# First attention: scores, maxima and exponentials for each head of a pair apart, with the query projection between the heads

## The chip, the cores and the metric

One core of a Trainium2 chip runs the whole program. The metric is the time of one execution on the device in microseconds; the kernel before took 1574.98 us (median of 3 runs, 1562.34 to 1577.71).

## The reference

Two transformer layers with adaptive layer norm on x of 8 x 256 x 128, all in float32. The change touches only the attention of the first layer: 16 heads of 64, in which every query sees 16 pooled keys (one for every segment of 16 tokens) and the keys of its own and the previous window of 128 tokens.

```
h = layernorm(x) * (1 + ca) + sa
q  = rotary(h @ w_q) * scale;  kv = rotary(h @ w_kv)
lkv = LN(kv windows, previous + own);  gkv = LN(softmax-pooled segments of kv)
sim = concat([mask(q @ gkv.T), mask(q @ lkv.T)], -1)
attn = softmax(sim, -1)
out = (attn @ concat([gkv, lkv])) @ w_out + b_out
x = x + ga * out
```

Behind it come a mixture of 4 experts (top 2), a second attention with relative positions, and a mixture of 16 experts (top 1).

## The kernel before, in words

The five engines have programs of their own, written out by hand, and meet by semaphores. The first attention works in slots, one for each of the 8 batches, plus two slots ahead of them. In a slot the 16 heads go in 8 pairs, `hp` 0 to 7. `n` is the number of the pair over all slots. The two heads of a pair, `e` 0 and 1, lie in partitions 0 to 63 and 64 to 127 of `qr` (rotated queries, two buffers) and `kT` (keys). Their scores go to the two banks of `S`, one bank for a head; `S` has no second buffer. For each of two query tiles `t` a row has 144 or 272 keys: 416 columns for a head.

In each engine's program the order is fixed:

- TensorE (`slot_program`, L549): `scores(n)` (L470; masks by an identity matmul in bf16, L478, then ten fp32 instructions, L483), the query projection of the next pair (`q_proj`, L460), a piece of other work that depends on `hp`, the values of pair n-2 (`av`, L502), the transposes of the probabilities of pair n-1 (`pT_tr`, L487), other work again. `hp` 2 has the output projection of the batch before, `hp` 3 the transposes of its normed rows (`h2T_mm`) and of the next batch but one (`hT_mm`), `hp` 4 and 5 the key and value projections, `hp` 6 and 7 the transposes of keys.
- VectorE (L998): the reciprocal of the sums of pair n-1 (L1010), the maxima of pair n (L1014, one instruction for both heads at each `t`), the rotation of the queries of pair n+1 (L1070, L1074), then work of other batches: statistics, norms, rotations, routing.
- ScalarE (L631): the normalisation of the probabilities of n-1 (L628), the four exponentials of n (L618), the copy of the values' result (L680), the copies of the transposed probabilities (L686, L687), other copies.
- POOL has the powers for the norms (L1127, L1181), the scaling of keys and values, and the scatter of rows.

`s_mm` counts finished scores, `s_max` finished maxima, `s_exp` finished exponentials. `scores(n)` waits for `q_sum` (the rotated queries) and for all four exponentials of pair n-1.

Of the kernel before, what the change touches and what calls it, by code (L numbers as in the profile page):

```python
# [24 lines left out]
ALU = mybir.AluOpType  # L25
ACT = mybir.ActivationFunctionType
X = mybir.AxisListType.X

P = 128
# [3 lines left out]
H0, DH0 = 16, 64  # L33
HP = H0 // 2
INNER = H0 * DH0
SEG = 16
NSEG = NT // SEG
# [10 lines left out]
KEYS = (NSEG + P, NSEG + 2 * P)  # L48
SCOLS = sum(KEYS)
S_AT = (KEYS[1], 0)  # L50
M_AT = (P, 0)
# [132 lines left out]
def layer0_attention(nc, io, keep):  # L184

    with ExitStack() as ctx:
# [13 lines left out]
        maskb = sb("maskb", [P, MCOLS], BF16)  # L200
        identb = sb("identb", [P, P], BF16)
# [48 lines left out]
        negmax = sb("negmax", [P, 2, TILES, 2])  # L250
# [28 lines left out]
        S = ctx.enter_context(nc.psum_tensor("S", [P, 2, 512], F32))  # L279
# [25 lines left out]
        s_mm = sem("s_mm"); s_max = sem("s_max"); s_exp = sem("s_exp")  # L305
# [5 lines left out]
        bank0 = Bank(sem("a0_full"), sem("a0_drained"), "lgT:E out:L h2T:L G:E kv00:N kv10:N kT1:E kT3:E pos:L")  # L311
        bank1 = Bank(sem("a1_full"), sem("a1_drained"), "pkT:E hT:N kv01:N router:L kv11:N gkT:E kT0:E kT2:E")
# [69 lines left out]
        def _(pe):  # L382
# [77 lines left out]
            def q_proj(n, b, bp, hp):  # L460
                if hp == 0:
                    pe.wait_ge(hq, b + 1)
                if not known_zero(n):
                    pe.wait_ge(q_rot, n)
                for s in range(2):
                    mm = pe.matmul(Q[:, s * NT:(s + 1) * NT], wq[:, s, hp * P:(hp + 1) * P], hT[:, bp, :],
                                   start=True, stop=True)
                mm.then_inc(q_mm, 1)

            def scores(n, b, bp, hp):  # L470
                if hp == 0:
                    bank1.wait_emptied(pe, "kT2", b - 1)
                    bank0.wait_emptied(pe, "kT3", b - 1)
                pe.wait_ge(q_sum, n + 1)
                if not known_zero(n):
                    pe.wait_ge(s_exp, 4 * n)
                for e, at in ((0, 0), (1, SCOLS - P)):
                    pe.matmul(S[:, e, M_AT[e]:SCOLS], identb[:], maskb[:, at:at + SCOLS - M_AT[e]], start=True, stop=False,  # L478
                              skip_group_check=True)
                for t, e, to, lo, w in ((1, 0, 0, NSEG, KEYS[1]), (1, 1, 0, 0, KEYS[1]), (0, 0, 0, NSEG, P), (0, 1, 0, 0, KEYS[0]),  # L480
                                        (0, 0, P, 0, NSEG)):
                    head = slice(e * DH0, (e + 1) * DH0)
                    mm = pe.matmul(S[:, e, S_AT[t] + to:S_AT[t] + to + w], qr[head, hp % 2, t * P:(t + 1) * P],  # L483
                                   kT[head, bp, hp, lo:lo + w], start=False, stop=(t == 0), skip_group_check=True)
                mm.then_inc(s_mm, 1)
# [63 lines left out]
            def slot_program(slot, bp):  # L549

                heads, early, late, norm = parts(slot)
                np_ = 1 - bp
                for hp in range(HP):
                    n = slot * HP + hp
                    last = heads if hp > 0 else late
                    if heads:
                        scores(n, slot, bp, hp)
                    if isinstance(slot, int) and slot == -1 and hp == HP - 1:
                        pe.wait_ge(wq_in, 16 * n_wq)
                        pe.wait_ge(cast, 2)  # L560
                        pe.wait_ge(set_up, PT_ZERO)
                    if hp < HP - 1 and heads:
                        q_proj(n + 1, slot, bp, hp + 1)
                    if hp == HP - 1 and early:
                        q_proj(n + 1, slot + 1, np_, 0)
                    if late and hp == 2:
                        out_mm(slot, slot - 1)
                    if early and hp == 4:
                        G_mm(slot, slot + 1)
                    if late and hp == 5:  # L570
                        router_mm(slot, slot - 1)
                    if early and hp == 6:
                        gkT_mm(slot, slot + 1)
                    if early and hp == 7:
                        for c in (2, 3):
                            kT_mm(slot, slot + 1, np_, c)
                    if (late if hp < 2 else heads):
                        av(n - 2, slot if hp > 1 else slot - 1, bp if hp > 1 else np_, (hp - 2) % HP)
                    if last:
                        pT_tr(n - 1, (hp - 1) % HP)  # L580
                    if early and hp == 0:
                        lgT_mm(slot, slot + 1)
                    if early and hp == 2:
                        pkT_mm(slot, slot + 1)
                    if late and hp == 3:
                        h2T_mm(slot, slot - 1)
                    if norm and hp == 3:
                        hT_mm(slot, slot + 2)
                    if norm and hp in (4, 5):
                        for k in range(2):  # L590
                            kv_mm(slot, hp - 4, k)
                    if early and hp == 6:
                        for c in (0, 1):
                            kT_mm(slot, slot + 1, np_, c)
                    if late and hp == 7:
                        pos_mm(slot, slot - 1)
# [9 lines left out]
        def _(act):  # L606
# [5 lines left out]
            act.copy(modT[:].rearrange("p m b -> p (m b)"), O[:, 0:2 * NB]).then_inc(modT_out, 1)  # L612

            def exponentials(n, hp):
                act.wait_ge(s_max, n + 1)
                for t in (1, 0):
                    for e in range(2):
                        act.activation(prob[:, hp % 2, prob_at(t, e):prob_at(t, e) + KEYS[t]],  # L618
                                       S[:, e, S_AT[t]:S_AT[t] + KEYS[t]], ACT.Exp,
                                       bias=negmax[:, hp % 2, t, e:e + 1],  # L620
                                       accum_out=Z[:, hp % 2, t, e:e + 1]).then_inc(s_exp, 1)
# [9 lines left out]
            def slot_program(slot, bp):  # L631
                heads, early, late, norm = parts(slot)
                np_ = 1 - bp
                b, l, r = slot + 1, slot - 1, slot + 2

                def keys_out(c):
                    bank, a = where[f"kT{c}"]
                    bank.wait_full(act, f"kT{c}", slot)
                    if c == 0 and not known_zero(b - 1):
                        act.wait_ge(s_mm, HP * (b - 1))  # L640
                    act.copy(kT[:, np_, 2 * c:2 * c + 2, NSEG:KEYS[1]],
                             a[:].rearrange("p (u k) -> p u k", u=2)).then_inc(bank.drained, 1)

                for hp in range(HP):
                    n = slot * HP + hp
# [13 lines left out]
                    if norm and hp in (5, 6):  # L659
                        t = hp - 5  # L660
# [51 lines left out]
        def _(dve):  # L712
# [30 lines left out]
            for l in range(2):  # L743
                dve.tensor_copy(modr[:, l, 0:384], (A0 if l == 0 else A1)[0:NB, 0:384])
                i = dve.tensor_copy(modr[:, l, 384:768], S[0:NB, l, 0:384])
# [136 lines left out]
            def pooled_keys(slot, b, bp):  # L882
                bank1.wait_full(dve, "gkT", slot)
                if not known_zero(b - 1):
                    dve.wait_ge(s_mm, HP * (b - 1))
                for at in (0, KEYS[1]):
                    for u in range(2):
                        i = dve.tensor_copy(kT[:, bp].rearrange("p (g u) k -> p g u k", u=2)[:, :, u, at:at + NSEG],
                                            A1[:, u * P:(u + 1) * P].rearrange("p (g s) -> p g s", g=4)[:, :, 0:NSEG])
                i.then_inc(bank1.drained, 1)  # L890
# [107 lines left out]
            def slot_program(slot, bp):  # L998
# [3 lines left out]
                for hp in range(HP):  # L1002
# [6 lines left out]
                            dve.wait_ge(p_norm, m - 1)  # L1009
                        dve.reciprocal(rZ[:, pb], Z[:, pb]).then_inc(z_recip, 1)  # L1010
                    if heads:
                        dve.wait_ge(s_mm, n + 1)
                        for t in (1, 0):
                            i = dve.tensor_reduce(negmax[:, hp % 2, t, :], S[:, :, S_AT[t]:S_AT[t] + KEYS[t]], X, ALU.max, negate=True)  # L1014
                        i.then_inc(s_max, 1)
                    if (heads if hp < HP - 1 else early):
                        rotate_queries(n + 1, (hp + 1) % 2)
                    if early and hp == 0:
# [46 lines left out]
            def rotate_queries(n, buf):  # L1065

                dve.wait_ge(q_mm, n + 1)
                if not known_zero(n):
                    dve.wait_ge(q_sum, n)
                dve.tensor_tensor(qt[:].rearrange("p s q -> p (s q)"), Q[:], cst("rotq"), ALU.mult).then_inc(q_rot, 1)  # L1070
                dve.wait_ge(q_rot, n + 1)
                if not (isinstance(n, int) and n < 2):
                    dve.wait_ge(s_mm, n - 1)
                dve.tensor_tensor(qr[:, buf, :], qt[:, 0, :], qt[:, 1, :], ALU.add).then_inc(q_sum, 1)  # L1074

            dve.wait_ge(const_in, 16)
# [1440 lines left out]
```

## Time and profile before

| | |
|---|---|
| median of 3 runs | 1574.98 us (1562.34 to 1577.71) |
| the profiled execution | 1569.16 us, span 1567.4 us |
| mean granted clock of TensorE | 0.88 |
| busy | TensorE 77%, weight loads 59%, VectorE 62%, ScalarE 52%, POOL 47% |
| VectorE waits for scores, 85 to 610 us | 82.0 us, 36 times |

Matmuls are pipelined and their ends are modelled, so that the start of the next instruction tells more than the length of one. An instruction of the language in fp32 is two of the profile's. A row merges consecutive instructions of one line; its shape is that of the first. P is the start of a pair's masks.

### The profile page before, as it was taken

The numbers are of one execution on the slowest core, as the hardware profiler recorded it, in microseconds if no ns is written. First come the engines' busy times: TensorE is split into PE (matmuls) and PEld (weight loads), VectorE is DVE, ScalarE is ACT, GpSimd is POOL, SyncE is SP. The second block draws the span as 40 slices with busy tenths as digits, with TensorE's granted clock in tenths as the row PEclk, the third lists the DMA queues.
The fourth block names the chain that finished last, engine by engine and source line by source line (L and its number), as shares of the span: only waits on it lengthen the run. The fifth ranks groups of instructions, "written<-read, shape, count | busy, mean of one in ns | idle before, by whom it ended". The sixth has DMA issues, their size and how long they took to land. (4 is left out here: it accounts for less than half of the span.)

```text
span 1567.4 us, 30063 instructions
## 1 busy us (share of the span) xinstructions
PE 1205.5 (77%) x9276; PEld 930.3 (59%) x9276; DVE 966.3 (62%) x2147; ACT 813.4 (52%) x2164; POOL 733.6 (47%) x732
## 2 busy tenths in 40 slices
PE   2268788977778897489889889889947987788436
PEld 0145555655555575389889889889933444444336
DVE  4586686877778753564754484474444577775633
ACT  1156565656657584366666666667622443333101
POOL 2646647383765611256556646556655233211223
PEclk7588898898989898699999999999977999888658
DMA  7500000000000000603000300000043365331135
GB/s 218 162 1 3 1 10 1 10 3 7 2 7 9 1 10 8 236 9 120 12 12 8 123 8 11 10 8 11 10 154 72 83 94 106 61 46 20 22 110 154
DMA packets 152775, 76.43 MB, mean 49 GB/s; under 512 B 99992, under 2 KB 143384, under 8 KB 152408
## 3 DMA queue, kind: packets, MB, share of 16 engines
q1 hardware_dynamic: 144696, 66.42, 16.3%
q0 software_dynamic: 3072, 6.31, 1.2%
q10 hardware_dynamic: 4896, 2.36, 0.5%
q8 instruction: 54, 0.88, 0.2%
q14 instruction: 57, 0.47, 0.1%
HBM read 54.77 MB, written 19.76 MB: 48 GB/s over the span
## 5 line engine op out<-in xcount | busy, mean ns | idle before, releaser
L1454 POOL TENSOR_TENSOR hl<-hid,hh 128x256 fp32r<-128x256 f32 x396 | 292.6, 741 | 224.1 <-ACT hh L1431 220.3
L1497 DVE SCALAR_TENSOR_TENSOR hid<-GU,gub,sg 128x256 f32<-128x256 f32 x396 | 190.3, 481 | 194.4 <-ACT sg L1425 114.7
L1325 PE MATMUL GU<-xh,wh 128*128 128x256 f32 x792 | 233.0, 294 | 42.6 <-DVE wl L1473 33.4
L1425 ACT ACTIVATE sg<-GU,gub 128x256 f32<-128x256 f32 x396 | 188.2, 475 | 121.9 <-PE GU L1327 120.4
L1326 PE MATMUL GU<-xl,wh 128*128 128x256 f32 x792 | 225.1, 284 | 0.0
L1327 PE MATMUL GU<-xh,wl 128*128 128x256 f32 x792 | 224.7, 284 | 0.0
L1325 PEld LDWEIGHTS GU<-xh,wh 128*128 128x128 f32 x792 | 151.6, 191 | 52.9 <-issue 27.8
L1431 ACT CAST hh<-hid 128x256 fp32r<-128x256 f32 x396 | 158.1, 399 | 29.7 <-DVE hid L1497 28.4
L1326 PEld LDWEIGHTS GU<-xl,wh 128*128 128x128 f32 x792 | 151.9, 192 | 0.0
L1327 PEld LDWEIGHTS GU<-xh,wl 128*128 128x128 f32 x792 | 151.9, 192 | 0.0
L628 ACT ACTIVATE prob<-prob,rZ 128x272 f32<-128x272 f32 (+1 forms) x256 | 98.9, 462 | 59.0 <-DVE rZ L1010 58.9
L1938 ACT ACTIVATE pT<-ST 128x1024 f32<-128x1024 f32 x64 | 65.5, 1023 | 111.5 <-PE ST L1768 111.5
L1325 PE MATMUL OUT<-hh,wh 128*128 128x256 f32 x396 | 113.6, 287 | 11.5 <-ACT yT L1397 10.5
L1014 DVE TENSOR_REDUCE negmax<-S 128x2 f32<-128x544 f32 (+1 forms) x128 | 69.0, 580 | 82.0 <-PE S L483 82.0
L618 ACT ACTIVATE prob<-S,negmax 128x272 f32<-128x272 f32 (+1 forms) x256 | 106.7, 426 | 22.0 <-DVE negmax L1014 21.9
L2061 DVE TENSOR_REDUCE top_now<-S 128x4 f32<-128x1024 f32 x64 | 78.2, 1223 | 55.4 <-PE S L1760 55.3
L1326 PE MATMUL OUT<-hl,wh 128*128 128x256 f32 x396 | 112.0, 283 | 0.0
L1327 PE MATMUL OUT<-hh,wl 128*128 128x256 f32 x396 | 111.8, 282 | 0.0
L1760 PE MATMUL S<-KA,QA 32*128 32x256 f32 x512 | 82.4, 444 | 13.6 <-DVE top_now L2061 10.5
L1325 PEld LDWEIGHTS OUT<-hh,wh 128*128 128x128 f32 x396 | 75.4, 190 | 15.1 <-POOL hl L1454 15.1
L1768 PE MATMUL ST<-QA,KA 32*128 32x256 f32 x512 | 83.0, 447 | 0.0
L1127 POOL TENSOR_TENSOR krs<-krs,half 128x32 f32<-128x32 f32 x8 | 43.7, 5458 | 81.2 <-DVE krs L815 81.2
(305 smaller groups left out, 2880.9 us busy)
## 6 DMA issues: line engine op xcount, KB each, us to landing
raw<-in_expert_w SPq DMA_DIRECT2D x4, 2688.0 KB, 12.3
late<-in_w SPq DMA_DIRECT2D x20, 256.0 KB, 6.3
raw<-in_expert_w SPq DMA_DIRECT2D x4, 1152.0 KB, 6.7
list<-zero SPq DMA_DIRECT2D x4, 1024.0 KB, 8.7
modb<-mod_d SPq DMA_DIRECT2D x9, 384.0 KB, 4.2
early<-rel_d SPq DMA_DIRECT2D x1, 3072.0 KB, 13.1
qkv_d<-qkv SPq DMA_DIRECT2D x48, 64.0 KB
early<-in_w SPq DMA_DIRECT2D x12, 256.0 KB, 4.2
```

The lines of the kernel that those rows point to most:

```text
L618: act.activation(prob[:, hp % 2, prob_at(t, e):prob_at(t, e) + KEYS[t]], S[:, e, S_AT[t]:S_AT[t] + KEYS[t]], ACT.Exp, bias=negmax[:, hp % ...
L628: i = act.activation(part, part, ACT.Copy, scale=rZ[:, pb, t, e:e + 1])
L1325: pe.matmul(out, lhs[0], rhs[0], start=start, stop=False, skip_group_check=True)
L1326: pe.matmul(out, lhs[0], rhs[1], start=False, stop=False, skip_group_check=True)
L1327: return pe.matmul(out, lhs[1], rhs[0], start=False, stop=stop, skip_group_check=True)
L1425: act.activation(sg[:, c % BUFS], GU[c % BUFS][:, 0:TT], ACT.Silu, bias=gub[:, GATE, e * CH0 + c:e * CH0 + c + 1]).then_inc(silu, 1)
L1431: act.copy(hh[:, d % BUFS], hid[:, d % BUFS]).then_inc(hid_hi, 1)
L1454: pool.tensor_tensor(hl[:, b], hid[:, b], hh[:, b].bitcast(F32), ALU.subtract).then_inc(hid_lo, 1)
L1497: dve.scalar_tensor_tensor(out=hid[:, c % BUFS], in0=GU[c % BUFS][:, TT:2 * TT], scalar=gub[:, UP, e * CH0 + c:e * CH0 + c + 1], in1=sg[:, ...
L1760: mm = pe.matmul(S[:, e, blk * NT:(blk + 1) * NT], QA[32 * j:32 * j + BLOCK, row % 2, g, blk * P:(blk + 1) * P], KA[32 * j:32 * j + BLOCK, ...
L1768: mm = pe.matmul(ST[:, e, blk * NT:(blk + 1) * NT], KA[32 * j:32 * j + BLOCK, row % 2, g, blk * P:(blk + 1) * P], QA[32 * j:32 * j + BLOCK ...
L2061: dve.tensor_reduce(to, S[:].rearrange("p e (q k) -> p e q k", q=2), X, ALU.max, negate=True).then_inc(s_max, 1)
```

## The change

The scores of a pair are computed for head 0 first (its mask, then 272, 128 and 16 columns), then the query projection of the next pair, then head 1 (mask, 272 and 144 columns). Each head waits only for the two exponentials of its own bank. VectorE takes four maxima for two, head by head, and ScalarE goes through the four exponentials head by head. `s_mm` and `s_max` rise by two for a pair.

```diff
@@ -467,19 +467,21 @@
                                    start=True, stop=True)
                 mm.then_inc(q_mm, 1)
 
-            def scores(n, b, bp, hp):
-                if hp == 0:
-                    bank1.wait_emptied(pe, "kT2", b - 1)
-                    bank0.wait_emptied(pe, "kT3", b - 1)
-                pe.wait_ge(q_sum, n + 1)
+            def scores(n, b, bp, hp, e):
+
+                if e == 0:
+                    if hp == 0:
+                        bank1.wait_emptied(pe, "kT2", b - 1)
+                        bank0.wait_emptied(pe, "kT3", b - 1)
+                    pe.wait_ge(q_sum, n + 1)
                 if not known_zero(n):
-                    pe.wait_ge(s_exp, 4 * n)
-                for e, at in ((0, 0), (1, SCOLS - P)):
-                    pe.matmul(S[:, e, M_AT[e]:SCOLS], identb[:], maskb[:, at:at + SCOLS - M_AT[e]], start=True, stop=False,
-                              skip_group_check=True)
-                for t, e, to, lo, w in ((1, 0, 0, NSEG, KEYS[1]), (1, 1, 0, 0, KEYS[1]), (0, 0, 0, NSEG, P), (0, 1, 0, 0, KEYS[0]),
-                                        (0, 0, P, 0, NSEG)):
-                    head = slice(e * DH0, (e + 1) * DH0)
+                    pe.wait_ge(s_exp, 4 * n - 2 + 2 * e)
+                at = (0, SCOLS - P)[e]
+                pe.matmul(S[:, e, M_AT[e]:SCOLS], identb[:], maskb[:, at:at + SCOLS - M_AT[e]], start=True, stop=False,
+                          skip_group_check=True)
+                head = slice(e * DH0, (e + 1) * DH0)
+                for t, to, lo, w in (((1, 0, NSEG, KEYS[1]), (0, 0, NSEG, P), (0, P, 0, NSEG)),
+                                     ((1, 0, 0, KEYS[1]), (0, 0, 0, KEYS[0])))[e]:
                     mm = pe.matmul(S[:, e, S_AT[t] + to:S_AT[t] + to + w], qr[head, hp % 2, t * P:(t + 1) * P],
                                    kT[head, bp, hp, lo:lo + w], start=False, stop=(t == 0), skip_group_check=True)
                 mm.then_inc(s_mm, 1)
@@ -554,7 +556,7 @@
                     n = slot * HP + hp
                     last = heads if hp > 0 else late
                     if heads:
-                        scores(n, slot, bp, hp)
+                        scores(n, slot, bp, hp, 0)
                     if isinstance(slot, int) and slot == -1 and hp == HP - 1:
                         pe.wait_ge(wq_in, 16 * n_wq)
                         pe.wait_ge(cast, 2)
@@ -563,6 +565,8 @@
                         q_proj(n + 1, slot, bp, hp + 1)
                     if hp == HP - 1 and early:
                         q_proj(n + 1, slot + 1, np_, 0)
+                    if heads:
+                        scores(n, slot, bp, hp, 1)
                     if late and hp == 2:
                         out_mm(slot, slot - 1)
                     if early and hp == 4:
@@ -612,9 +616,9 @@
             act.copy(modT[:].rearrange("p m b -> p (m b)"), O[:, 0:2 * NB]).then_inc(modT_out, 1)
 
             def exponentials(n, hp):
-                act.wait_ge(s_max, n + 1)
-                for t in (1, 0):
-                    for e in range(2):
+                for e in range(2):
+                    act.wait_ge(s_max, 2 * n + e + 1)
+                    for t in (1, 0):
                         act.activation(prob[:, hp % 2, prob_at(t, e):prob_at(t, e) + KEYS[t]],
                                        S[:, e, S_AT[t]:S_AT[t] + KEYS[t]], ACT.Exp,
                                        bias=negmax[:, hp % 2, t, e:e + 1],
@@ -637,7 +641,7 @@
                     bank, a = where[f"kT{c}"]
                     bank.wait_full(act, f"kT{c}", slot)
                     if c == 0 and not known_zero(b - 1):
-                        act.wait_ge(s_mm, HP * (b - 1))
+                        act.wait_ge(s_mm, 2 * HP * (b - 1))
                     act.copy(kT[:, np_, 2 * c:2 * c + 2, NSEG:KEYS[1]],
                              a[:].rearrange("p (u k) -> p u k", u=2)).then_inc(bank.drained, 1)
 
@@ -882,7 +886,7 @@
             def pooled_keys(slot, b, bp):
                 bank1.wait_full(dve, "gkT", slot)
                 if not known_zero(b - 1):
-                    dve.wait_ge(s_mm, HP * (b - 1))
+                    dve.wait_ge(s_mm, 2 * HP * (b - 1))
                 for at in (0, KEYS[1]):
                     for u in range(2):
                         i = dve.tensor_copy(kT[:, bp].rearrange("p (g u) k -> p g u k", u=2)[:, :, u, at:at + NSEG],
@@ -1009,10 +1013,11 @@
                             dve.wait_ge(p_norm, m - 1)
                         dve.reciprocal(rZ[:, pb], Z[:, pb]).then_inc(z_recip, 1)
                     if heads:
-                        dve.wait_ge(s_mm, n + 1)
-                        for t in (1, 0):
-                            i = dve.tensor_reduce(negmax[:, hp % 2, t, :], S[:, :, S_AT[t]:S_AT[t] + KEYS[t]], X, ALU.max, negate=True)
-                        i.then_inc(s_max, 1)
+                        for e in range(2):
+                            dve.wait_ge(s_mm, 2 * n + e + 1)
+                            for t in (1, 0):
+                                i = dve.tensor_reduce(negmax[:, hp % 2, t, e:e + 1], S[:, e, S_AT[t]:S_AT[t] + KEYS[t]], X, ALU.max, negate=True)
+                            i.then_inc(s_max, 1)
                     if (heads if hp < HP - 1 else early):
                         rotate_queries(n + 1, (hp + 1) % 2)
                     if early and hp == 0:
@@ -1070,7 +1075,7 @@
                 dve.tensor_tensor(qt[:].rearrange("p s q -> p (s q)"), Q[:], cst("rotq"), ALU.mult).then_inc(q_rot, 1)
                 dve.wait_ge(q_rot, n + 1)
                 if not (isinstance(n, int) and n < 2):
-                    dve.wait_ge(s_mm, n - 1)
+                    dve.wait_ge(s_mm, 2 * (n - 1))
                 dve.tensor_tensor(qr[:, buf, :], qt[:, 0, :], qt[:, 1, :], ALU.add).then_inc(q_sum, 1)
 
             dve.wait_ge(const_in, 16)
```

On TensorE, in the last slot, whose pairs have nothing else between them: the instructions from one pair's scores on. Before:

```order
L478 MATMUL S<-maskb,identb 128x288 [waits s_exp,q_sum]
L478 MATMUL S<-maskb,identb 128x416
L483 MATMUL S<-kT,qr 128x272 x2
L483 MATMUL S<-kT,qr 128x128
L483 MATMUL S<-kT,qr 128x144
L483 MATMUL S<-kT,qr 128x16
L466 MATMUL Q<-hT,wq 128x256 [waits q_rot]
L466 MATMUL Q<-hT,wq 128x256
```

And now:

```order
L480 MATMUL S<-maskb,identb 128x288 [waits s_exp,q_sum]
L485 MATMUL S<-kT,qr 128x272
L485 MATMUL S<-kT,qr 128x128
L485 MATMUL S<-kT,qr 128x16
L466 MATMUL Q<-hT,wq 128x256 [waits q_rot]
L466 MATMUL Q<-hT,wq 128x256
L480 MATMUL S<-maskb,identb 128x416 [waits s_exp]
L485 MATMUL S<-kT,qr 128x272
L485 MATMUL S<-kT,qr 128x144
```

The matmuls are the same ones. Those of the two heads alternated; now the projection stands between them, and head 1 has a wait of its own.

On VectorE, at the same place of the last slot, before:

```order
L1010 RECIPROCAL rZ<-Z 128x4 [waits p_norm,s_exp]
L1014 TENSOR_REDUCE negmax<-S 128x2 [waits s_mm]
L1014 TENSOR_REDUCE negmax<-S 128x2
L1070 TENSOR_TENSOR qt<-Q,const 128x512 [waits q_sum,q_mm]
L1074 TENSOR_TENSOR qr<-qt 128x256 [waits s_mm,q_rot]
```

And now:

```order
L1014 RECIPROCAL rZ<-Z 128x4 [waits p_norm,s_exp]
L1019 TENSOR_REDUCE negmax<-S 128x1 [waits s_mm]
L1019 TENSOR_REDUCE negmax<-S 128x1
L1019 TENSOR_REDUCE negmax<-S 128x1 [waits s_mm]
L1019 TENSOR_REDUCE negmax<-S 128x1
L1075 TENSOR_TENSOR qt<-Q,const 128x512 [waits q_sum,q_mm]
L1079 TENSOR_TENSOR qr<-qt 128x256 [waits s_mm,q_rot]
```

The rotation of the next pair's queries, and whatever VectorE has behind it, stands behind the maximum of head 1.

## Rows read from the trace of the kernel before

**Rows 1.** The page, section 1: busy time, share of the span, instructions.

```profile
PE 1205.5 (77%) x9276; PEld 930.3 (59%) x9276; DVE 966.3 (62%) x2147; ACT 813.4 (52%) x2164; POOL 733.6 (47%) x732
```

**Rows 2.** Waits, 85 to 610 us: us in total, times, longest.

```profile
DVE negmax L1014 <- PE S L483: 82.0, 36, 7.2
...
ACT prob L618 <- DVE negmax L1014: 21.9, 18, 9.8
...
PE S L478 <- ACT prob L618: 1.9, 5, 0.8
```

**Rows 3.** Timeline of TensorE, slot 7: start, us, operation [idle before].

```profile
583.31 0.46 PE L478 MATMUL S<-maskb,identb 128*128 128x288 bf16 x2
583.70 1.07 PE L483 MATMUL S<-kT,qr 64*128 64x272 f32 x10
584.70 1.13 PE L466 MATMUL Q<-hT,wq 128*128 128x256 f32 x4
585.76 0.69 PE L509 MATMUL O<-pT,gv 32*128 32x256 f32 x2
...
588.12 0.29 PE L478 MATMUL S<-maskb,identb 128*128 128x288 bf16 x1
```

**Rows 4.** The same in instants of 0.01 us, at 583.75, 584.10 and 585.30.

```profile
583.70 0.50 PE L483 MATMUL S<-kT,qr 64*128 64x272 f32 x2
...
583.70 0.73 PE L483 MATMUL S<-kT,qr 64*128 64x272 f32 x4
...
585.02 0.59 PE L466 MATMUL Q<-hT,wq 128*128 128x256 f32 x2
```

**Rows 5.** Timeline of VectorE, the same pair.

```profile
584.81 1.09 DVE L1014 TENSOR_REDUCE negmax<-S 128x2 f32<-128x544 f32 x2 [1.75 <-PE S L483]
585.87 0.69 DVE L1070 TENSOR_TENSOR qt<-Q,const 128x512 f32<-128x512 f32 x1
```

**Rows 6.** Busy time of the engines in that period, granted clock, DMA, GB/s.

```profile
583.31:588.12 4.81, 4.81 (x37) 3.35 (x35) 2.36 (x5) 4.35 (x16) 0.00 (x0) 1.00 0.00 0
```

**Rows 7.** VectorE's groups by shape, 85 to 612 us: busy us, mean ns.

```profile
L1014 DVE TENSOR_REDUCE negmax<-S 128x2 f32<-128x544 f32 x64 | 45.7, 714 | 82.0 <-PE S L483 82.0
...
L1014 DVE TENSOR_REDUCE negmax<-S 128x2 f32<-128x288 f32 x64 | 28.6, 446 | 0.0
```

**Rows 8.** Timeline of TensorE, slot 5, pairs 2 to 5.

```profile
443.71 0.47 PE L478 MATMUL S<-maskb,identb 128*128 128x288 bf16 x2 [0.28 <-ACT prob L618]
...
452.42 0.47 PE L478 MATMUL S<-maskb,identb 128*128 128x288 bf16 x2
...
465.15 0.68 PE L530 MATMUL A<-const,h 128*128 128x128 f32 x2 [7.75 <-DVE h L929]
...
466.06 0.79 PE L478 MATMUL S<-maskb,identb 128*128 128x288 bf16 x2
...
475.38 0.46 PE L478 MATMUL S<-maskb,identb 128*128 128x288 bf16 x2
```

**Rows 9.** Timeline of VectorE, slot 5, pairs 3 to 5.

```profile
457.34 3.59 DVE L923 TENSOR_SCALAR h<-x,mv,rs 128x128 f32 x2 [0.58 <-POOL rs L1181]
...
468.76 1.09 DVE L1014 TENSOR_REDUCE negmax<-S 128x2 f32<-128x544 f32 x2 [3.65 <-PE S L483]
...
476.88 1.09 DVE L1014 TENSOR_REDUCE negmax<-S 128x2 f32<-128x544 f32 x2 [3.84 <-PE S L483]
```

**Rows 10.** Timeline of POOL, slot 5, pair 2 to pair 3.

```profile
451.03 5.54 POOL L1127 TENSOR_TENSOR krs<-krs,half 128x32 f32<-128x32 f32 x1 [10.00 <-DVE krs L815]
```

**Rows 11.** Timelines of TensorE and VectorE, slot 5, pair 6.

```profile
482.25 0.46 PE L478 MATMUL S<-maskb,identb 128*128 128x288 bf16 x2
...
485.95 0.69 DVE L1014 TENSOR_REDUCE negmax<-S 128x2 f32<-128x544 f32 x1
```

**Rows 12.** Busy time in two stretches behind stalls; the clock stands before DMA.

```profile
466.00:468.80 2.80, 2.80 (x15) 1.91 (x12) 0.04 (x1) 2.26 (x6) 2.80 (x2) 0.50 0.00 0
...
292.80:297.00 4.20, 4.20 (x14) 2.23 (x14) 3.44 (x7) 3.19 (x12) 2.80 (x3) 0.50 0.08 33
```

## The prediction

> **What bounds the kernel now.** I read the page first: TensorE is the busiest engine, 77% of the 1567.4 us span [rows 1]. The change touches the first attention alone, roughly 85 to 610 us, so every other number comes from there. There the list of waits comes next: VectorE waits 82.0 us in 36 waits for the scores, ScalarE 21.9 us for the maxima, and TensorE's wait for the exponentials, the one that the ring is about, is 1.9 us in 5 waits [rows 2]. So the ring of scores, maxima and exponentials is closed by TensorE arriving late far more often than by TensorE being held.
>
> The timeline of one pair shows why. Call P the start of a pair's mask matmuls; here P is 583.31, and the next P is 588.12, so the period is 4.81 us [rows 3]. TensorE has no idle row in it: masks and scores to 584.70, query projection to 585.76, values and transposes to 588.12. It is busy for all 4.81 us at a granted clock of 1.00, which is 2.4 GHz, with ScalarE at 4.35 us [rows 6]. VectorE waited 1.75 us for these scores, its maximum starts at P+1.50, its rotation at P+2.56 [rows 5].
>
> The third thing to see is how the scores stream. The two heads lie in different halves of the partitions, and their matmuls run together: just after 583.70 two instructions are in flight and end within 0.50 us; four are through in 0.73. Two of the query projection, which uses all 128 rows, take 0.59 [rows 4]. So a step of 272 columns costs 0.73-0.50 = 0.23 us for both heads, about what 256 columns of one query projection instruction cost: 585.02+0.59 to 584.70+1.13, 0.22 us [rows 3, 4].
>
> The Trainium skill, in TensorEngine Tiling (Array Packing), Key Properties, says that different tiles of the array work in parallel; the trace agrees with those 0.23 us.
>
> **TensorE, per pair.** The change puts the query projection between the heads, so no score matmul has a partner. Now both heads together take 583.70 to 584.70, 1.00 us [rows 3]: 0.33 for the first step, 0.23 for its second half, two steps of 128 to 144 columns at about 0.12, and 0.19 for the rest and the emptying. A head alone has the same steps (272, 128 and 16 columns, or 272 and 144) and takes about 0.97. Two heads: 1.94, **+0.94**. A second passage from mask to scores (0.39 from the first mask to the scores, 0.29 of it columns at 2.4 GHz [rows 3]) adds 0.10; a mask behind the projection, of the same array shape, saves about that much. No row has 272 columns of one head alone: the bounds are half the pair's step (+0, if one head could stream twice as fast) and the projection's rate (+0.94). I take the upper, since a projection instruction is the nearest row.
>
> The same page says that changing the tiling mode drains the engine. The change has four such passages per pair in place of three; the page gives no time, and by that rule alone the sum would be +0.1 per pair.
>
> **VectorE.** Head 0's maximum can start early, at about P+1.3. Head 1's scores are ready at P+0.22 (first mask) +0.97+0.96 (projection) +0.27 (second mask) +0.97+0.11 = P+3.50 in place of P+1.50. The maxima now take 714 and 446 ns for 544 and 288 elements [rows 7], 1.05 ns per element; 272 and 144 elements are then 0.43 and 0.29, 0.62 with the overlap that the pair has now. The rotation starts at P+4.12 in place of 2.56: **+1.56** wherever VectorE waits for the scores. Everything behind it on VectorE waits as well. Where it comes late anyway, it pays two more instructions: 4 by 0.36 against 1.16, less two overlaps of 0.10, +0.1 to 0.2; I take 0.15. ScalarE's eight activations are the same; head 0's exponentials are earlier, head 1's end near P+5.0, in front of the new P+5.75. The added semaphore steps cost nothing that a row shows.
>
> **A whole slot** (eight pairs; the example is slot 5). Pairs are 0 to 7.
> - P of pair 2 was held 0.28 us by the exponentials [rows 8]. This wait goes: +0.94-0.28 = +0.66.
> - P2 to P3 (443.71 to 452.42) is the output projection and the rest on TensorE without a wait: +0.94.
> - P3 to P4: TensorE waits 7.75 us for the rows of the second norm [rows 8]. VectorE is late by 1.56, but idled 0.58 there for POOL's power [rows 9], which stands behind a power of 5.54 us [rows 10], itself late by what pair 2 is late: +0.98.
> - P4 to P5 (466.06 to 475.38): VectorE idles 3.65 and 3.84 us for the scores [rows 9], TensorE paces it: +0.94.
> - P5 to its rotation: +1.56.
> - Pairs 6, 7 and 0: pair 6's P is 482.25, VectorE comes at 485.95 [rows 11]. Head 1 would be ready at 485.75, and VectorE itself comes 1.56 later: hidden. Without that cover it would be 1.56 again. Left is 3 x 0.15 = +0.45.
>
> Sum: 0.66+0.94+0.98+0.94+1.56+0.45 = 5.53 us. Slots 1 to 6 make 33.2; slot 0, less regular, I take as another 5.5; slot 7 has no fill work, eight pairs by 0.94 = 7.5. Together **+46 us**. Against the profiled execution's own 1569.16 us that is 1615. That run lies 0.4% below the median of the runs, 1574.98; I add a little for that and say **1617**.
>
> **The rivals.**
> - *The ring pays (faster).* If the early maximum of head 0 lets ScalarE start sooner and one head streams at the pair's whole rate, the 21.9 us that ScalarE waits for maxima and the 2 to 3 us of TensorE's ring wait [rows 2] come back: 1569-24 = 1545. It decides as soon as ScalarE sets the period. For: ScalarE is at 4.35 of 4.81 us [rows 6]. Against: TensorE has none left at all, and head 1's maximum comes later than now, ring or not. Chance 0.05.
> - *No change.* A head alone streams twice as fast (the lower bound), head 0's early work repays the switches: 1560 to 1585. Chance 0.07.
> - *Most of it is absorbed.* VectorE's delay is taken up by its idle stretches of 3.65 and 3.84 us [rows 9], and only TensorE's own stretches count: P2 to P3 and P4 to P5 in seven slots, 13 us, and slot 7, 7.5: 1590. Against: those idle stretches end with the very scores that come late. Chance 0.13.
> - *The low clock doubles it.* Behind each long stall TensorE runs at 0.50, 1.2 GHz (466.0 to 468.8), and once for 4.2 us on end [rows 12]. If scores spread over more of it, pair 4 or pair 0 pays twice, +3 to 4 us in six or seven slots: 1640. Chance 0.13.
> - *As summed*: 1617, own range 1600 to 1632. Chance 0.62.
>
> The range of 8 in 10 leaves out the first two rivals and the far end of the fourth: 1588 to 1640. A measurement of this kernel tells about 1% from no change. Faster by over 1%: 0.05; within 1%: 0.07 and a tenth of the third, 0.08; slower: 0.87.
>
> **What would show it.** In the changed profile: query projection starts at about P+1.2 and the second mask at P+2.15; the values' first matmul at P+3.4 where it was at P+2.45; the period of slot 7's plain pairs near 5.75 for 4.81; two score instructions of 272 columns never in flight together. VectorE's maxima: 128 of about 0.43 and 128 of about 0.29 us, with a new wait of 1.5 us between the heads, and its waits for scores well above 82 us. P3 to P4 longer by 1, pairs 6 and 7 hardly changed. I would be wrong if a head alone streamed 272 columns in 0.12 us, if slot 7's period stayed under 5 us, or if time outside 85 to 610 us moved.

## The result, and the profile after

The changed kernel takes **1680.2 us** (median of 4 runs, 1665.3 to 1691.8) against 1573.9 us (median of 4 by now): ratio 1.0668, 95% interval 1.0614 to 1.0722. The forecast was 1617 us, with 1588 to 1640 as the range. The direction was right and the size not: +106 us where +46 had been summed. The profiled execution took 1674.99 us, its span is 1673.2 us.

The page, section 1, against [rows 1]:

```profile
PE 1321.2 (79%) x9276; PEld 1002.4 (60%) x9276; DVE 992.9 (59%) x2275; ACT 817.8 (49%) x2164; POOL 733.8 (44%) x732
```

TensorE is busy 116 us longer with the same 9276 matmuls. Next the pair by which the price was worked out, in slot 7, TensorE and then VectorE, against [rows 3] and [rows 5] (start, us, operation):

```profile
671.37 0.29 PE L480 MATMUL S<-maskb,identb 128*128 128x288 bf16 x1
671.59 1.07 PE L485 MATMUL S<-kT,qr 64*128 64x272 f32 x6
672.59 1.13 PE L466 MATMUL Q<-hT,wq 128*128 128x256 f32 x4
673.56 0.34 PE L480 MATMUL S<-maskb,identb 128*128 128x416 bf16 x1
673.83 0.97 PE L485 MATMUL S<-kT,qr 64*128 64x272 f32 x4
674.73 0.69 PE L511 MATMUL O<-pT,gv 32*128 32x256 f32 x2
...
677.08 0.29 PE L480 MATMUL S<-maskb,identb 128*128 128x288 bf16 x1
```

```profile
674.83 0.66 DVE L1019 TENSOR_REDUCE negmax<-S 128x1 f32<-128x272 f32 x2 [0.44 <-PE S L485]
675.40 0.68 DVE L1075 TENSOR_TENSOR qt<-Q,const 128x512 f32<-128x512 f32 x1
```

P is 671.37 and the period is 5.71 us; 4.81 before, 5.75 forecast. The values begin at P+3.36 (3.39 was summed), head 1's maximum at P+3.46 (3.50), the rotation at P+4.03 (4.12). Head 0's three score matmuls take 1.00 us, and head 1's two 0.90; before, both heads took 1.00 together. So at the full clock the model of one pair was right.

In this pair head 0's maximum waits until P+2.36 (673.73). That is the exception: in pairs 2 to 6 of slot 7 it comes at P+1.32 to P+1.33, with a wait of 1.48 us between the heads, where 1.3 and 1.5 were forecast. The next pair, with P at 677.08:

```profile
678.41 0.66 DVE L1019 TENSOR_REDUCE negmax<-S 128x1 f32<-128x272 f32 x2 [1.73 <-PE S L485]
680.54 0.66 DVE L1019 TENSOR_REDUCE negmax<-S 128x1 f32<-128x272 f32 x2 [1.48 <-PE S L485]
```

Now the two stretches that it missed. Slot 4, pairs 3 and 4, TensorE, against [rows 8], which are of slot 5 (slot 5 of the changed kernel has the same rows 83.25 us later, to 0.01 us, up to the end of the stall):

```profile
443.82 0.30 PE L480 MATMUL S<-maskb,identb 128*128 128x288 bf16 x1
...
461.53 0.69 PE L532 MATMUL A<-const,h 128*128 128x128 f32 x2 [11.83 <-DVE h L933]
...
462.43 0.45 PE L480 MATMUL S<-maskb,identb 128*128 128x288 bf16 x1
...
466.55 0.55 PE L480 MATMUL S<-maskb,identb 128*128 128x416 bf16 x1
...
476.60 0.29 PE L480 MATMUL S<-maskb,identb 128*128 128x288 bf16 x1
```

The stall is 11.83 us for 7.75. The second mask comes 4.12 us behind the first; in slot 7 it was 2.19. This is the low clock: over slot 5's P4 to P5 its mean is 0.53.

```profile
545.69:560.88 15.19, 15.19 (x56) 8.67 (x54) 3.27 (x9) 6.49 (x19) 3.49 (x2) 0.53 0.00 0
```

VectorE and POOL in that stall, against [rows 9] and [rows 10]:

```profile
449.02 3.68 DVE L779 TENSOR_SCALAR h<-xt,mv,rs 128x128 f32 x2
452.62 3.80 DVE L927 TENSOR_SCALAR h<-x,mv,rs 128x128 f32 x2
```

```profile
442.78 5.43 POOL L1132 TENSOR_TENSOR krs<-krs,half 128x32 f32<-128x32 f32 x1 [16.80 <-DVE krs L819]
448.18 0.69 POOL L1186 TENSOR_TENSOR rs<-rs,half 128x2 f32<-128x2 f32 x1
448.84 3.78 POOL L1141 TENSOR_TENSOR V<-kvc,krs 128x1024 f32<-128x1024 f32 x2
```

The two small norm instructions of L779 begin at 449.02, 0.18 us behind POOL's scaling of V. Before (slot 5), they stood in front of it and took 0.59 us for two:

```profile
456.17 0.59 DVE L775 TENSOR_SCALAR h<-xt,mv,rs 128x128 f32 x2
```

```profile
457.09 3.75 POOL L1136 TENSOR_TENSOR V<-kvc,krs 128x1024 f32<-128x1024 f32 x2
460.81 3.93 POOL L1154 TENSOR_TENSOR wk<-kvr,pk 128x1024 f32<-128x1024 f32 x2
```

The Trainium skill, GPSIMD Engine Reference, Specifications, says that POOL shares its SBUF interfaces with VectorE, with contention for VectorE instructions in a 2-port mode or with two inputs from SBUF. The trace agrees for the norm's two-input steps of 128x256, which took 2.34 us beside POOL's work and 0.43 away from it. The one-input steps took 3.68 us for two against 0.59; whether they ran in such a mode no run here shows. The rows show one thing more: beside POOL, a step lasts about as long as one instruction of POOL's, 1.88 us where POOL's two scalings of V take 3.78, and 2.34 where the next two take 4.82.

Last the clock, over all 64 pairs, of the kernel before and of the changed one (first to last P; the clock stands before DMA):

```profile
85.24:598.08 512.84, 419.66 (x2755) 293.01 (x2755) 383.01 (x785) 331.65 (x1040) 279.37 (x165) 0.90 0.02 5
```

```profile
84.78:711.15 626.37, 541.08 (x2754) 367.94 (x2755) 410.93 (x911) 336.75 (x1040) 278.30 (x165) 0.80 0.01 4
```

A mean of 0.80 over 626 us between two levels, 0.5 and 1, is 2 x 0.20 x 626 = 251 us at 1.2 GHz; before it was 2 x 0.10 x 513 = 103 us. The trace's clock records add up to 253 and 105, and these are used from here on. Not all of that time is a loss, since TensorE stands idle in part of it. Laid over its busy records, it worked for 202 us at 1.2 GHz, and for 70 before. Half of that is what the clock took, by estimate 101 us and 35, so 66 us more than before. Some of this hides behind waits. From first to last P the loss is 113.5 us; 7 us of it come back behind the last pair.

P to P, mean of slots 1 to 5, in us (read from the timelines of TensorE):

| | 0-1 | 1-2 | 2-3 | 3-4 | 4-5 | 5-6 | 6-7 | 7-0 | sum |
|---|---|---|---|---|---|---|---|---|---|
| before | 8.58 | 6.12 | 8.76 | 13.62 | 9.38 | 6.87 | 7.28 | 9.02 | 69.6 |
| changed | 9.79 | 6.79 | 9.80 | 18.60 | 14.65 | 8.09 | 7.57 | 8.92 | 84.2 |
| added | 1.21 | 0.67 | 1.04 | 4.98 | 5.27 | 1.22 | 0.29 | -0.10 | 14.6 |
| forecast | 0.15 | 0.66 | 0.94 | 0.98 | 0.94 | 1.56 | 0.15 | 0.15 | 5.5 |

Two of eight intervals hold 8.3 of the 9.1 us that the forecast lacks in each slot. Slots 0 and 6 look different: slot 0 grew by 14.2 us and slot 6 by 19.3, and in slot 6 pairs 1 and 2 hold 11.6 of them (P1 to P3 25.1 us for 13.5) and P3 to P4 only 0.6. Slot 7 grew by 7.15 us, where 7.5 were forecast.

### The profile page after: what moved, and what is told of

It reads as the page before. It is cut to its first block and busy times, and to the rows that moved or that the text cites. A ratio compares the mean times of both kernels' runs of the same rounds, so it can differ in the third digit from the quotient of the medians.

```text
span 1673.2 us, 30311 instructions
## 1 busy us (share of the span) xinstructions
PE 1321.2 (79%) x9276; PEld 1002.4 (60%) x9276; DVE 992.9 (59%) x2275; ACT 817.8 (49%) x2164; POOL 733.8 (44%) x732
## 3 DMA queue, kind: packets, MB, share of 16 engines
q1 hardware_dynamic: 144696, 66.42, 15.2%
q10 hardware_dynamic: 4896, 2.36, 0.5%
## 5 line engine op out<-in xcount | busy, mean ns | idle before, releaser
L1019 DVE TENSOR_REDUCE negmax<-S 128x1 f32<-128x272 f32 (+1 forms) x256 | 82.1, 366 | 189.9 <-PE S L485 189.9
L485 PEld LDWEIGHTS S<-kT,qr 64*128 64x128 f32 x640 | 119.0, 220 | 66.6 <-issue 48.8
L485 PE MATMUL S<-kT,qr 64*128 64x272 f32 (+3 forms) x640 | 157.4, 380 | 0.0
L1330 PE MATMUL OUT<-hh,wh 128*128 128x256 f32 x396 | 113.5, 287 | 10.8 <-ACT yT L1402 9.8
```

The lines of the kernel that those rows point to most:

```text
L1019: i = dve.tensor_reduce(negmax[:, hp % 2, t, e:e + 1], S[:, e, S_AT[t]:S_AT[t] + KEYS[t]], X, ALU.max, negate=True)
L1330: pe.matmul(out, lhs[0], rhs[0], start=start, stop=False, skip_group_check=True)
```

## The experiments

There are 4 to 10 runs of each. The ratio is to the kernel before, run beside it (medians of 1567.6 to 1573.9 us). "1.2 GHz" is the time at the lower level from first to last P, and "working" the part of it in which TensorE was busy, both in us and both from the one profiled execution; the last column is slot 7's plain period. In the edits `...` marks what is left out.

| kernel | us | ratio (95%) | 1.2 GHz | working | period |
|---|---|---|---|---|---|
| before | 1573.9 | 1 | 105 | 70 | 4.81 |
| changed | 1680.2 | 1.0668 (1.0614 to 1.0722) | 253 | 202 | 5.71 |
| e1_grouped | 1611.0 | 1.0252 (1.0195 to 1.0308) | 173 | 141 | 5.27 |
| e2_pe_only | 1708.1 | 1.0865 (1.0826 to 1.0905) | 290 | 230 | 6.56 |
| e3_split_vector | 1573.3 | 1.0001 (0.9966 to 1.0036) | 139 | 104 | 4.81 |
| e4_partners | 1637.5 | 1.0402 (1.0333 to 1.0470) | 126 | 73 | 5.72 |
| e5_before_warm | 1551.3 | 0.9915 (0.9876 to 0.9953) | 59 | 52 | 4.81 |
| e6_after_warm | 1662.4 | 1.0560 (1.0479 to 1.0640) | 155 | 147 | 5.71 |
| e7_after_early_norm | 1662.4 | 1.0572 (1.0487 to 1.0657) | 232 | 202 | 5.71 |
| e8_after_early_norm_warm | 1635.7 | 1.0415 (1.0336 to 1.0493) | 134 | 129 | 5.71 |
| e9_after_early_norm_warm8 | 1614.7 | 1.0266 (1.0209 to 1.0322) | 88 | 82 | 5.71 |
| e10_before_hold | 1564.5 | 0.9958 (0.9925 to 0.9991) | 117 | 97 | 4.81 |
| e11_before_hold_weigh | 1568.4 | 0.9964 (0.9927 to 1.0001) | 110 | 100 | 4.81 |
| e12_after_hold_weigh | 1619.4 | 1.0317 (1.0257 to 1.0378) | 154 | 145 | 5.71 |

### Which part of the change costs

**e1_grouped**

```diff
-for t, e, to, lo, w in ((1, 0, 0, NSEG, KEYS[1]), (1, 1, 0, 0, KEYS[1]), (0, 0, 0, NSEG, P), (0, 1, 0, 0, KEYS[0]), (0, 0, P, 0, NSEG)):
+for t, e, to, lo, w in ((1, 0, 0, NSEG, KEYS[1]), (0, 0, 0, NSEG, P), (0, 0, P, 0, NSEG), (1, 1, 0, 0, KEYS[1]), (0, 1, 0, 0, KEYS[0])):
```

> The kernel before, with one change: behind both masks, head 0's three score matmuls are issued in a row and then head 1's two, with the query projection behind them as before. Theory (the two heads stream together only while their matmuls alternate): scores take 1.7 us in place of 1.0, slot 7's plain period goes from 4.81 to about 5.5 us, the whole is slower by 4 to 6%. Rival (the place of the query projection is what costs): period 4.8, no change. Rival (a head alone streams at the pair's rate): no change.

The same matmuls in another order cost 2.5%. In slot 7 the scores take from 634.36 to 635.82:

```profile
634.36 1.54 PE L483 MATMUL S<-kT,qr 64*128 64x272 f32 x10
635.82 1.13 PE L466 MATMUL Q<-hT,wq 128*128 128x256 f32 x4
```

That is 1.46 us for 1.00. I had expected 1.7: I had counted nothing of head 1 that can run beside head 0's last matmuls, and its first, of 272 columns, starts 0.01 us behind head 0's of 128, at 634.93. The ratio fell short of the 4 to 6% as well. The alternation is worth 0.46 us per pair without the query projection, and both rivals fall. The changed kernel's period is 0.44 us longer still: with the projection between the heads nothing of head 1 runs beside head 0 at all.

**e2_pe_only**

```diff
-pe.wait_ge(s_exp, 4 * n - 2 + 2 * e)
+pe.wait_ge(s_exp, 4 * n)
...
-for e in range(2):
-    dve.wait_ge(s_mm, 2 * n + e + 1)
-    for t in (1, 0): dve.tensor_reduce(negmax[:, hp % 2, t, e:e + 1], S[:, e, ...])
+dve.wait_ge(s_mm, 2 * n + 2)
+for t in (1, 0): dve.tensor_reduce(negmax[:, hp % 2, t, :], S[:, :, ...])
```

(and the exponentials in the order of before)

> The changed kernel's TensorE program with the maxima, exponentials and waits of the kernel before (two maxima for both heads, when both are ready). Theory (all of the loss comes from TensorE's scores without a partner): within 1.5% of the changed kernel, 1665 to 1700 us, slot 7's period 5.7. Rival (the split of maxima and exponentials on VectorE and ScalarE carries a good part): well below, about 1620.

Slower even than the changed kernel, with a period of 6.56 for 5.71 us. TensorE's new order is the whole loss, and more: the split on the other engines wins back 1.8%. The size was missed, 1708 for at most 1700, and the period most of all. In slot 7 TensorE now stands idle in front of the masks until the pair before has its exponentials, which it did not in the changed kernel:

```profile
702.31 0.28 PE L480 MATMUL S<-maskb,identb 128*128 128x288 bf16 x1 [0.69 <-ACT prob L622]
```

Once the scores come late, it pays to start on head 0 early.

**e3_split_vector** (the kernel before; only the maxima, exponentials and their semaphores are apart, and head 0's matmul of 16 columns goes in front of head 1's last one)

```diff
+if t == 0 and (to or e):
+    mm.then_inc(s_mm, 1)
...
-dve.wait_ge(s_mm, n + 1)
+for e in range(2):
+    dve.wait_ge(s_mm, 2 * n + e + 1)
...
```

> The kernel before, with only the split on VectorE and ScalarE: each head's two maxima and two exponentials apart, the matmuls of both heads still alternating and the projection behind them. Theory: 0.15 us more on VectorE per pair where it paces, so 1575 to 1590 us. Rival (the ring of one head apart is worth something): 1545 to 1565.

No change, 1.0001, with an interval of 0.35% to each side, some 6 us: two more reductions per pair and the heads' exponentials apart cost or win nothing that can be told, at least taken together. TensorE still waits for all four exponentials here, so that this half of the ring is not tested by e3.

### Are half-filled matmuls free to pair, and what do they do to the clock

**e4_partners** (on the changed kernel; the partner's result is overwritten, and its wait for O stands ahead of head 1's scores)

```diff
                     mm = pe.matmul(S[:, e, ...], qr[head, ...], kT[head, ...], ...)
...
+                    if partner:
+                        other = slice((1 - e) * DH0, (2 - e) * DH0)
+                        pe.matmul((Q, O)[e][:, 0:w], qr[other, ...], kT[other, ...], start=True, stop=True)
```

> The changed kernel, and behind every score matmul one of the same columns on the other head's 64 rows, whose result goes to a free bank and is overwritten. Theory (two row halves stream together, and the low clock lasts longer because half of the array stands idle): slot 7's period stays near 5.7 us although there is twice the score work, TensorE's mean granted clock between 85 us and the end of the attention goes back up from 0.80 towards 0.90, and the time falls below the changed kernel's, to 1610 to 1640. Rival (the clock is low for the longer stalls alone): clock still 0.80, 1675 to 1695. Rival (they do not stream together): period 7 us, over 1720.

Twice the score matmuls, and the period stays at 5.72 us. TensorE's timeline there:

```profile
655.25 0.49 PE L488 MATMUL S<-kT,qr 64*128 64x272 f32 x1
655.26 0.49 PE L492 MATMUL Q<-kT,qr 64*128 64x272 f32 x1
655.59 0.39 PE L488 MATMUL S<-kT,qr 64*128 64x272 f32 x1
655.60 0.39 PE L492 MATMUL Q<-kT,qr 64*128 64x272 f32 x1
```

Each partner starts 0.01 us behind its matmul and the next step comes no later than without it. And the kernel with more work is 2.5% **faster** than the changed one. The stretch 93 to 150 us, of the kernel before, of the changed one and then of this one:

```profile
93.00:150.00 57.00, 45.50 (x276) 29.76 (x276) 34.53 (x67) 36.24 (x114) 35.03 (x20) 0.87 0.01 2
```

```profile
93.00:150.00 57.00, 53.70 (x194) 33.89 (x195) 27.01 (x60) 28.08 (x84) 28.09 (x14) 0.59 0.00 1
```

```profile
93.00:150.00 57.00, 48.31 (x300) 32.00 (x300) 29.39 (x74) 33.14 (x100) 33.15 (x19) 0.83 0.01 2
```

The changed kernel has TensorE busy for 53.70 of 57 us, at a mean clock of 0.59; with partners it is 0.83. P4 to P5 goes from 14.65 to 10.61 us while P3 to P4, with the stall, stays at 18.61. TensorE works 73 us at 1.2 GHz where it was 202. So of the 106 us some 43 go when the other half of the array works beside the scores, and the low clock goes with them. What of the array's activity the clock answers to is not settled by this.

### The stall and the clock behind it

**e5_before_warm** and **e6_after_warm** (12 in place of 8; none in the last slots)

```diff
+bank, a = use("h2T", slot)
+for k in range(8 ...):
+    pe.matmul(a[:], ident, wq[:, 0, 0:512], start=True, stop=True, ...)
 pe.wait_ge(h2_done, b + 1)
-bank, a = use("h2T", slot)
```

> The kernel before, with 8 matmuls of constants (512 columns, fp32, result overwritten) on TensorE in the stall of pair 3, in front of its wait for the rows of the second norm; none in the last slots. Theory (idling there brings the low clock, which lasts into pair 4): P4 to P5 shrinks from 9.4 to about 8 us, low clock between 85 us and the last pair falls well below its 106 us, the time by 5 to 15 us, to 1558 to 1568. Rival (the clock falls for another reason): 1573, clock as before, or slower where the filling overruns the stall.

> The changed kernel with 12 such matmuls in the same place, where its stall is 11.8 us. Theory (a good part of the loss is the low clock behind the longer stall): P4 to P5 falls from 14.6 to about 10 us, low clock from 256 us to under 150, and the time by 25 to 45 us, to 1635 to 1655. Rival (the clock is low because the scores use half of the array, whatever went before): low clock stays over 200 us, time within 1%.

On the kernel before: P4 to P5 is 7.55 us for 9.38, at a clock of 1.00, and the kernel is 0.85% faster. No other version beats the kernel before by as much, and this one does it by matmuls whose result nobody reads. On the changed kernel P4 to P5 falls from 14.65 to 9.62 (8.45 in four of the five slots, at a clock of 1.00). Slot 5:

```profile
533.30:541.75 8.45, 8.45 (x57) 5.17 (x54) 3.17 (x9) 5.92 (x19) 3.99 (x2) 1.00 0.00 0
```

So at the full clock this interval costs 8.45 - 7.55 = 0.90 us more than in the kernel before, and 0.94 was forecast. The time, though, falls only by 1%, less than expected, and the two intervals of the ratio overlap. In the profiled execution the lower clock came up elsewhere in exchange, in pairs 1 to 4 of slot 3: P1 to P2 is 10.66 and P2 to P3 13.91 us, where slots 1, 2, 4 and 5 have 5.7 to 5.8 and 9.8. So TensorE still works 147 us at 1.2 GHz, for 202.

### The collision

**e7_after_early_norm**

```diff
                         residual(slot, l)
+                    if norm and hp == 2:
...
+                        layernorm1_end(r)
...
-                    if norm and hp == 3:
...
-                        layernorm1_end(r)
```

> The changed kernel with the two small norm instructions of the next batch (h from xt, each 0.35 us in the kernel before and 1.88 in the changed one) at the end of pair 2 on VectorE, before the maxima of pair 3, in place of behind its rotation. Theory (VectorE came so late that they fell under POOL's scaling of V, which slows them fivefold): they take 0.35 us again, P3 to P4 falls from 18.6 to about 15.5 us, the stall with it, the time by 15 to 35 us, to 1645 to 1665. Rival (P3 to P4 is longer for the wait between the heads alone): 18 us, under 1% less.

```profile
431.19 0.60 DVE L779 TENSOR_SCALAR h<-xt,mv,rs 128x128 f32 x2
```

The two take 0.60 us again, and P3 to P4 is 14.00 for 18.60. The 4.6 us are the 3.68 that no longer stand there, and most of the rest the two-input steps behind, which take 1.90 and 1.89 us in place of 2.34 and 2.33: they run beside POOL's weighing (3.94 us for two instructions) and no longer beside the next step on V (4.82 for two). Of the 4.98 us that the interval had grown by, 0.4 are left. P4 to P5 is 15.2 for 14.65, and in slots 3 and 6 the low clock shows where the changed kernel had none (P1 to P2 9.85 for 5.72, P5 to P6 11.61 for 6.64), which keeps the gain at 1%. Taken alone it lies within the noise, as that of e6 does; e8 and e9, with both edits, are clear of it.

**e8_after_early_norm_warm** and **e9_after_early_norm_warm8** are both edits (early norm and filling) together, with 12 and 8 filling matmuls.

> Both of the last two on the changed kernel: early norm and 12 matmuls in the stall (now about 8.7 us, so the filling overruns it a little). Theory (what then is left is what was forecast: the scores without a partner and VectorE's later maximum): 1610 to 1635. Rival (clock and collision have little to do with it): over 1660.

> The changed kernel with the early norm and 8 filling matmuls for 12, so that they end inside the stall of about 7.5 us. Theory (12 overran it, P3 to P4 was 16.5 us with them and 14.0 without): P3 to P4 near 14 us, P4 to P5 near 8.5, the time 10 to 20 us below the version with 12, 1615 to 1630, which is what was forecast for the change. Rival (the rest of the loss is something else): 1635 or more.

With 12, P3 to P4 is 16.46 us, held by the filling itself; with 8 it is 13.54. P4 to P5 is then 9.26, where 8.5 was expected. In slot 4 the clock there is 1.00, and TensorE waits 0.54 us for a step of VectorE's on the pooled keys, which no term had. The kernel with e9's edits takes **1614.7 us**. Its two edits take out what the forecast's sum had not in it, and what is left is 2.7% above the kernel before; the forecast had 46 of 1569, 2.9%. Part of that agreement is luck: the filling gains on the kernel before as well. Against e5, which has it, e9 is 3.5% slower (1.0266 to 0.9915), 55 us. Of these the low clock can hold some 15, since TensorE works 82 us at 1.2 GHz in e9 and 52 in e5, and half of the difference is lost.

**e10_before_hold**, **e11_before_hold_weigh** and **e12_after_hold_weigh** (the latter on the changed kernel)

```diff
 if early and hp == 3:
+    if late:
+        pool.wait_ge(h2_done, l + 1)
     normalise(b, np_)
     if not known_zero(b):
         weigh(slot, b)
```

and in the latter two, besides:

```diff
-    normalise(b, np_)
     if not known_zero(b):
         weigh(slot, b)
+    normalise(b, np_)
```

> The kernel before, where POOL waits with its scaling of V and weighing until VectorE has finished the rows of the second norm, so that the two do not run at once. Theory (POOL's two-input work slows VectorE's norm instructions three to five times): the four norm steps of pair 3 take about 1.6 us for 7.4, P3 to P4 falls from 13.6 to about 8 us; POOL is 2 us later and the pooled keys' matmuls wait for it, so P4 to P5 grows by about 2: 1545 to 1560. Rival (POOL's own chain is what counts): 1575 to 1600.

> The same, and POOL weighs the pooled keys before it scales V, since the matmuls of pair 4 wait for the former. Theory: nothing waits in pair 4, 1530 to 1550. Rival (the scaled V is late for pair 6's transposes): no better than the version before it.

> The changed kernel with both of these POOL edits. Theory (collision and low clock added to the price of the split; without the long stall they go): 1585 to 1620, a distance of 50 to 70 us to the kernel before with the same edits. Rival (the distance of 106 us is independent of them): 1635 or more.

With POOL waiting 2.13 us for VectorE, the norm steps in e10 are quick, then TensorE waits for POOL instead:

```profile
454.44 0.61 DVE L923 TENSOR_SCALAR h<-x,mv,rs 128x128 f32 x2 [0.58 <-POOL rs L1181]
455.19 0.43 DVE L927 TENSOR_TENSOR h<-h,modb 128x256 f32<-128x256 f32 x1
```

```profile
456.35 3.76 POOL L1136 TENSOR_TENSOR V<-kvc,krs 128x1024 f32<-128x1024 f32 x2 [2.13 <-DVE h L929]
```

```profile
464.14 1.96 PE L439 MATMUL A<-wk,const 128*32 128x256 f32 x16 [4.80 <-POOL wk L1154]
```

L923 takes 0.61 for 3.59 us [rows 9], and P3 to P4 is 7.20 for 13.62. But P4 to P5 is 15.98 for 9.38. With the weighing first (e11) that is 8.68, and the wait moves on: P5 to P6 is 9.25 for 6.87, P6 to P7 11.21 for 7.28. It is not V that TensorE waits for there, as I had expected, but the pooled keys, which POOL scales behind V (waits, 85 to 600 us):

```profile
PE A L447 <- POOL gk L1167: 23.4, 7, 5.2
```

Neither gains 1%; I had expected up to 2.5%. POOL's own chain is nearly as long as VectorE's: in the kernel before its weighing ends at 464.74, 0.4 us before the stall does. What VectorE's slow norm cost there by itself is not shown, since both edits pay for the quick norm by holding POOL back. In the changed kernel the same edits bring 1680 to 1619 us, and its distance to the kernel before with the same edits is 3.5% (1.0317 against 0.9964), not 6.7%: the same 3.5% as between e9 and e5.

## Why the prediction was wrong, point by point

- **What bounds the kernel, and the two heads streaming together**: right. e1 shows that order alone is worth 0.46 us per pair, and e4 that a partner costs no time.
- **TensorE, +0.94 per pair**: right, 0.90 in the plain pairs. The lower bound, a head alone at twice the rate, is ruled out.
- **VectorE, +1.56, and the ends for P2 to P3 and P1 to P2**: right in slot 7, 1.47; P5 to P6, where it was to show in full, grew by 1.22. P2 to P3 +1.04 for 0.94. That P1 to P2 grew by 0.67 for 0.66 is luck: the low clock makes it 5.2 to 7.8 us before and 5.7 to 10.5 after.
- **P3 to P4, +0.98**: this step failed; the interval grew by 4.98. It moved the norm instructions by 1.5 us and kept their durations. The row of POOL's power [rows 10] was read for its end, not for what POOL does next. Starting 0.18 us behind the scaling of V, two instructions took 3.68 for 0.59 us; e7 gives 4.6 us back in this interval in each of slots 1 to 5, 23 us in all.
- **P4 to P5, +0.94**: this step failed too; the interval grew by 5.27. It priced pair 4 at the full clock once that had come back as quickly as before. The stall was longer and the scores were of one head at a time, and the lower clock held on; with partners the interval is 4.0 us shorter, with the filling 5.0. At the full clock the price was right, 0.90 (e6 against e5).
- **The rival of the low clock** was the right mechanism at too small a price: +23 us on top, where e4 wins back 43. It assumed doubled pairs 4 and 0; the time at 1.2 GHz rose from 105 to 253 us, in pairs 1 to 3 and all through slot 0 too, which grew by 14 us for 5.5, and slot 6 grew by 19.
- **P0 to P1, +0.15**: 1.21. With the partners it is 8.56, as before the change, which points to the clock here too; from slot to slot it runs from 7.0 to 11.4 us, so that no more can be read from the mean.
- **Absorbed, no change, the ring pays**: all wrong. e3 prices the heads' maxima and exponentials apart at nothing within 6 us. In the new order they are worth 1.8% (e2), but that only softens the loss.
- **The sum for full clock and no collision**: 46 us forecast. The kernels with these two taken out on both sides are 55 us apart (e9 against e5, e12 against e11); that e9's 1614.7 us meets the 1617 so closely is in part luck.

What is open: why the lower clock appears in pairs 1 to 3 of some slots and not of others, and how much the long stall and the one-headed scores each have in it. e4 alone gives 43 us; e6 and e7 alone give 18 each, or 17 and 15 by their ratios, at the edge of the noise; and they overlap. e4 adds rows, columns and instructions at once, so that it does not tell which of them the clock went with.

## What to carry to other kernels

Where two matmuls use different halves of the array's rows, their order is part of their price: alternate them, and put nothing that uses all rows between. Before a delay is priced by moving instructions along the time axis, look at what the other engines do at the new place, POOL above all, since a duration read at the old place does not move with the instruction. And a longer stall on TensorE, or work on half of its rows, can have a second price behind it in the granted clock: here partners alone won back 43 us, beside the 46 that were forecast.

## What the runs showed of the hardware

- Score matmuls of the two heads start 0.01 us apart and end together; a partner on the other 64 rows added no time to a 272-column step.
- TensorE can be busy 53.7 of 57 us and be granted a mean clock of 0.59; with the other half of the rows in use as well it was 0.83, and 0.87 in the kernel before. More work made the kernel 43 us faster.
- One-input norm instructions of 128 columns on VectorE took 1.88 us beside POOL's scaling of V and 0.34 to 0.35 alone; two-input ones of 256 columns took 1.9 to 2.3 us beside POOL's work and 0.43 alone. Each lasted about as long as one of POOL's instructions beside it. Beside POOL's power of 5.4 to 5.5 us they were not slowed (the kernel before: 0.59 us for two one-input steps at 456.17 and 0.43 for a two-input one at 451.54, with the power running from 451.03 to 456.57 [rows 10]).
- Eight matmuls of constants in a stall of TensorE's made the kernel before 0.85% faster: the pair behind the stall ran at a clock of 1.00 and took 7.55 us for 9.38.
